# Fewer semaphore updates in a graph network's edge loops, one core of Trainium2

## Chip, cores and metric

One core of a Trainium2 chip runs the whole program as one launch. The metric is the device time of an execution in microseconds (us). The kernel before takes 5689.62 us, the median of three runs (5685.16 to 5692.77). In the text PE is the matrix engine (TensorE), DVE VectorE, ACT ScalarE, POOL GpSimd, SP the engine that starts most plain transfers.

## What is computed

A network of four parts on 3125 nodes with 256 features each. Two of them go over edges:

```python
def _L0_gnn_ref(...):                      # 50000 edges, weight edge_val
    support = input_feature @ weight
    messages = edge_val[:, None] * support[edge_col]
    return segment_sum(messages, edge_row, N_NODES) + bias

def _gat_conv(x, src, dst, W, a_src, a_dst, b, n_nodes):   # edges and one loop a node
    h = (x @ W).reshape(n_nodes, H, C)
    e = leaky_relu((h * a_src).sum(-1)[src] + (h * a_dst).sum(-1)[dst], 0.2)
    ex = exp(e - segment_max(e, dst)[dst])
    alpha = ex / (segment_sum(ex, dst)[dst] + 1e-16)
    return segment_sum(h[src] * alpha[:, :, None], dst).reshape(n_nodes, H * C) + b
```

The first graph layer is a weighted sum over edges. The first feed-forward part chooses among four experts by scores that come from an attention layer of the same form (4 heads, width 16: the "gate"). Then come three attention layers (4 heads of 64) and a last feed-forward part with eight experts. Each part has a layer norm ahead of it and is added to its input.

## The kernel before

The edges are first sorted by destination on the chip (place_edges, place_fine), so that 128 edges at a time, a chunk or column, belong to one bucket of destination nodes. For each column a small table in SBUF holds the number of its bucket.

**sum_edges** (L610) goes over 415 chunks. For each, POOL gathers 128 rows of the table with an indirect transfer (L651) into one of 16 buffers (RS); DVE writes a one-hot matrix times the edge weights (mark, L625) into one of 8 buffers (PS); PE multiplies them (L662) into one of 8 PSUM buffers; DVE adds the result to the bucket's sum in `acc` (take, L631), whose address is a number that DVE loads into a register. Three semaphores say how far each is: `hot` (marks), `summed` (matmuls), `taken` (takes), one update each a chunk. POOL waits for `summed` before it gathers into a buffer again.

**attend_edges** (L665) is the loop of all four attention stages: 72 quads in the gate, 114 in each of the three layers, 414 in all. A quad is four columns (QD = 4). Each engine has its own program, written out in the order in which it runs; a loop body holds six quads (U = 6), with six buffers for gathered rows. For quad q:

- POOL waits until the quad's indices are copied (`staged`) and until quad q - 5 is summed, notes each wait by an own update (`passed`), then issues four gathers (L709).
- DVE fence (L728): waits for ACT's mask, the landed rows and PE's `turned`; subtracts the mask from the rows' scores. The result marks which destination each edge has.
- PE turn (L870): four transposes, then `turned`.
- DVE L757 reduces them to a maximum for each column; L763 scans it to a running maximum, L769 and L774 turn that into the exponent's shift `neg`, L778 into `drop`, by how much an older sum must shrink. Each waits for the one before by `steps`. In between stand the four add_up (L743) of quad q - 2: `acc` times the shrinking factor plus the quad's sums, each waiting for the one before by `taken`, at an address from a loaded bucket number (load_buckets, L732).
- ACT lift (L821): adds the destination's score to the four blocks; stage (L807): copies the indices of quad q + 6; fence (L814): four masks for quad q + 2.
- DVE leak (L748): the leaky relu.
- ACT weigh: four exponentials (L831), each with its own update of `exped`, and a fifth small one (L832), the shrinking factor, with `shrunk`.
- PE turn_back (L878): four transposes, each waiting for its exponential, each with its own update of `turned2`.
- ACT back (L838): waits for all four, copies them from PSUM (`evacd`).
- PE add_rows (L886): 16 small matmuls of weights and gathered rows (each two records in the trace, so x32), then `summed`.

DVE runs fence(q + 1) before the reduce of q; PE runs turn(q + 1) before turn_back(q) and add_rows(q). A stage ends with quads for which POOL has nothing more to gather. No scheduler decides anything: the order on each engine is that of the code.

Of the kernel before, what the change touches and what calls it, by code (L numbers as in the profile page):

```python
# [5 lines left out]
P = 128  # L6
N = 3125
D = 256
# [11 lines left out]
GROUP = 24  # L20
DB = 32
# [111 lines left out]

def place_edges(nc, block, m, name, key_in, val_in, w_in, rec_dram, record, row, bucket):
# [45 lines left out]
    def _(dve):  # L180
# [53 lines left out]
        chain.next(nc.vector.tensor_copy(bucket, ps_bucket))  # L234


def place_fine(nc, block, m, name, key_in, val_in, nch, record, bucket, own_hot, starts, trip_count):
# [45 lines left out]
    def _(dve):  # L283
# [75 lines left out]
        nc.vector.tensor_copy(bucket, ps_bucket)  # L359
        chain.next(nc.vector.tensor_scalar(starts, ps_start, -BIG, None, ALU.mult))  # L360
# [249 lines left out]
def sum_edges(nc, block, m, name, table, rec, index, bucket):  # L610


    hot, summed, taken, cleared = (m.sem(f"{name}_{s}") for s in ("hot", "summed", "taken", "cleared"))
# [4 lines left out]
    part = rec.rearrange("p (c k) -> p c k", k=3)  # L618

    @block.vector  # L620
    def _(dve):
        def mark(c):
            if c >= PS:
                dve.wait_ge(summed, c - PS + 1)
            nc.vector.tensor_scalar(f.hot[c % PS][:, :], m.iota[:, :], part[:, c, 0:1], part[:, c, 2:3], ALU.is_equal, ALU.mult).then_inc(hot, 1)  # L625

        def take(c, b):
            dve.wait_ge(summed, c + 1)
            if c:
                dve.wait_ge(taken, c)  # L630
            nc.vector.tensor_tensor(m.acc[:, b, 0:D], m.acc[:, b, 0:D], ps[c % PS], ALU.add).then_inc(taken, 1)  # L631

        nc.vector.memset(m.acc[:, :, :], 0.0).then_inc(cleared, 1)
        dve.wait_ge(cleared, 1)
        for c in range(PS):
            mark(c)
        for c in range(NCS):
            if c % 4 == 0:
                n = min(4, NCS - c)
                b = nc.values_load_multi_w_load_instructions(bucket[0:1, c:c + n], [mybir.EngineType.DVE], min_val=0, max_val=NT,  # L640
                                                             skip_runtime_bounds_check_because="a bucket's number counts up to 25 buckets")[1]
            take(c, b[c % 4])
            if c + PS < NCS:
                mark(c + PS)

    @block.gpsimd
    def _(pool):
        for c in range(NCS):
            if c >= RS:
                pool.wait_ge(summed, c - RS + 1)  # L650
# [5 lines left out]
    def _(pe):  # L656
        for c in range(NCS):
            pe.wait_ge(hot, c + 1)
            if c >= PS:
                pe.wait_ge(taken, c - PS + 1)  # L660
            pe.wait_ge(landed[c % RS], 16 * (c // RS + 1))
            nc.tensor.matmul(ps[c % PS], f.hot[c % PS][:, :], f.rows[c % RS][:, :], start=True, stop=True).then_inc(summed, 1)  # L662


def attend_edges(nc, block, m, name, width, table, at_dram, nch, lows, rows_in, bucket, own_hot, starts, trip_count):  # L665
# [9 lines left out]
    passed, staged, fenced, masked, turned, reduced, lifted, leaked, top, exped, shrunk, turned2, evacd, summed, taken, steps, acc_in, at_in, tabled, ready = (  # L675
        s_(n) for n in ("passed", "staged", "fenced", "masked", "turned", "reduced", "lifted", "leaked", "top", "exped", "shrunk", "turned2", "evacd", "summed", "taken", "steps",
# [24 lines left out]
    def _(pool):  # L701
        def gather(q, s, first=False):
            pool.wait_ge(staged, q + 1)
            pool.sem_inc(passed, 1)
            if not first:
# [15 lines left out]
    def _(dve):  # L721
        def fence(q, s, turn):

            dve.wait_ge(fenced, q + 1)
            dve.wait_ge(landed[s], turn * (16 * QD) + 16 * QD)
            if not isinstance(q, int) or q >= 2:
                dve.wait_ge(turned, q + (-1))
# [3 lines left out]
        def load_buckets(q):  # L731
            return nc.values_load_multi_w_load_instructions(bucket[0:1, bass.ds(q * QD, QD)], [mybir.EngineType.DVE], min_val=0, max_val=NS - 1,  # L732
                                                            skip_runtime_bounds_check_because="a bucket's number is a sum of one-hot rows times 0 to 99")[1]

        def add_up(q, s, t, b):
            if t == 0:
                dve.wait_ge(shrunk, q + 1)
                dve.wait_ge(summed, q + 1)
            if isinstance(q, int) and q == 0 and t == 0:
                dve.wait_ge(acc_in, 16 * HEADS)  # L740
            if not isinstance(q, int) or q or t:
                dve.wait_ge(taken, q * QD + t)
            nc.vector.scalar_tensor_tensor(acc[:, b, :], acc[:, b, :], f.fac[s][:, t:t + 1], ps_s[s % 2][:, t, :], ALU.mult, ALU.add).then_inc(taken, 1)  # L743
# [6 lines left out]
        def body(q, k, turn, last=None):  # L750
# [8 lines left out]
            if before:  # L759
                add_up(q + (-2), s2, 0, b[0])  # L760
# [3 lines left out]
                                         running[:, bass.ds(q * (2 * QD), 1)], ALU.add, ALU.max).then_inc(steps, 1)  # L764
            if before:
                add_up(q + (-2), s2, 1, b[1])
            neg = f.neg[k]
            dve.wait_ge(steps, q * 3 + 1)
            nc.vector.scalar_tensor_tensor(neg, now.rearrange("p (t k) -> p t k", k=2), -1.0,  # L769
                                           dst[:, bass.ds(q * QD, QD)].unsqueeze(2).to_broadcast([P, QD, 2]), ALU.mult, ALU.subtract).then_inc(steps, 1)  # L770
            if before:
                add_up(q + (-2), s2, 2, b[2])
            dve.wait_ge(steps, q * 3 + 2)
            nc.vector.scalar_tensor_tensor(neg, neg, 0.2, neg, ALU.mult, ALU.min).then_inc(steps, 1)  # L774
            if before:
                add_up(q + (-2), s2, 3, b[3])
            dve.wait_ge(steps, q * 3 + 3)
# [819 lines left out]
```

## Time and profile before

| | us |
|---|---|
| median of 3 runs | 5689.62 (5685.16 to 5692.77) |
| the profiled execution | 5690.18 |
| its span, first to last instruction | 5688.4 |
| PE busy | 2952.8 (52%) |
| DVE busy | 3228.2 (57%) |
| ACT busy | 1883.2 (33%) |
| POOL busy | 2839.1 (50%) |
| mean granted clock of PE | 0.627 |

In time, sum_edges lies at about 1117 to 1716 us (its gathers L651 start from 1117.4 to 1704.4), the gate's loop at about 1836 to 2325, the three layers' loops at about 2800 to 3570, 3665 to 4433 and 4526 to 5296. The sort of the edges comes ahead, the experts between the gate and the first layer and at the end.

How to read the rows further below: a timeline row has the start, the duration, engine, line, operation and tiles, and in brackets how long the engine stood idle ahead of it and what ended that. "remote" stands for a semaphore whose update the trace can't put down to an instruction on this core, "issue" for nothing visible. In a group's row the idle time ahead of all its instructions is added up.

### The profile page before, as it was taken

Reading aid. Unit: us, or ns where it says so; the run is one execution under the profiler, and the core shown is the slowest. Engines: PE = TensorE matmul, PEld = TensorE weight load, DVE = VectorE, ACT = ScalarE, POOL = GpSimd, SP = SyncE. Lnnn points to the kernel's source line nnn. Section 1 sums busy time; section 2 is a strip of 40 time slices with the busy share of each in tenths; the row PEclk is TensorE's granted clock in tenths of the full one; section 3 lists DMA queues with packets and bytes.
Section 4 is the critical chain, followed back from the end, with each engine's and each line's share of the span. In section 5 each row is a group of like instructions: output and inputs, shape, how many; then the busy total and the mean of one; then the engine's idle time right before and its main releaser. Section 6 shows DMA issues by size and latency. Waiting matters only on the chain. (4 is left out here: it accounts for less than half of the span.)

```text
span 5688.4 us, 84219 instructions
## 1 busy us (share of the span) xinstructions
PE 2952.8 (52%) x22141; PEld 1795.1 (32%) x22141; DVE 3228.2 (57%) x8605; ACT 1883.2 (33%) x6577; POOL 2839.1 (50%) x2704
## 2 busy tenths in 40 slices
PE   0235038676554444699455555455555555555274
PEld 0111001133232222477233333333333333333153
DVE  8799999844444444422455555455555455555815
ACT  0000000000001566311266666266666356566310
POOL 2877987266660666100266665166666156665010
PEclk9678569855665555799655555655555655555587
DMA  1000000123331000000333333333333333333000
GB/s 63 27 1 4 0 1 2 50 91 93 93 91 10 8 7 7 19 17 0 80 82 82 82 82 79 77 81 82 81 82 81 69 88 82 82 82 82 9 17 24
DMA packets 201198, 297.75 MB, mean 52 GB/s; under 512 B 110659, under 2 KB 140318, under 8 KB 201022
## 3 DMA queue, kind: packets, MB, share of 16 engines
q0 software_dynamic: 108656, 245.98, 17.4%
q1 hardware_dynamic: 92398, 50.07, 3.5%
q8 instruction: 63, 1.03, 0.1%
q14 instruction: 81, 0.66, 0.0%
HBM read 272.84 MB, written 23.05 MB: 52 GB/s over the span
## 5 line engine op out<-in xcount | busy, mean ns | idle before, releaser
L709 POOL DMA_INDIRECT work<-table_att,work x1368 | 1380.1, 1009 | 1588.5 <-ACT work L807 727.1
L757 DVE TENSOR_REDUCE work<-psum 128x512 f32 (+1 forms) x414 | 286.2, 691 | 1124.6 <-remote 1122.3
L886 PE MATMUL psum<-work 128*32 128x65 f32 (+1 forms) x13248 | 418.3, 295 | 947.4 <-ACT work L838 935.0
L418 POOL DMA_INDIRECT sorted<-stage_rec,stage_row x400 | 675.1, 1688 | 177.1 <-issue 124.0
L878 PE MATMUL psum<-ident,work 128*128 128x128 f32 x1656 | 559.3, 474 | 375.4 <-ACT work L831 278.5
L886 PEld LDWEIGHTS psum<-work 128*32 128x32 f32 x13248 | 331.0, 165 | 1067.6 <-issue 976.9
L831 ACT ACTIVATE work<-work 128x128 f32<-128x128 f32 x1656 | 530.0, 390 | 131.8 <-issue 102.0
L493 ACT ACTIVATE stats<-stats 128x25 f32<-128x25 f32 x5 | 1.1, 223 | 1690.5 <-DVE stats L483 1690.5
L651 POOL DMA_INDIRECT work<-table_sum,index x415 | 395.8, 954 | 278.2 <-SPq L1495 86.1
L838 ACT COPY work<-psum 128x512 f32<-128x512 f32 x414 | 242.2, 585 | 846.2 <-remote 664.6
L821 ACT ACTIVATE work<-psum,work 128x128 f32<-128x128 f32 x1656 | 472.3, 368 | 147.5 <-DVE work L757 130.8
L878 PEld LDWEIGHTS psum<-ident,work 128*128 128x128 f32 x1656 | 301.4, 182 | 677.7 <-ACT work L831 401.3
L662 PE MATMUL psum<-work 128*128 128x256 f32 x830 | 367.0, 572 | 258.8 <-DVE work L625 146.7
L743 DVE SCALAR_TENSOR_TENSOR acc<-acc,work,psum 128x65 f32 (+1 forms) x1656 | 445.9, 269 | 75.5 <-issue 10.8
L870 PE MATMUL psum<-ident,work 128*128 128x128 f32 x1656 | 462.4, 434 | 37.1 <-DVE work L728 28.5
L709 POOL DMA_INDIRECT work<-table_gate,work x288 | 293.4, 1019 | 306.3 <-ACT work L807 131.9
L397 PE MATMUL psum<-work 128*128 128x504 f16 (+1 forms) x1312 | 364.2, 361 | 98.1 <-DVE work L381 41.1
L814 ACT ACTIVATE work<-iota,lows 128x32 f32<-128x32 f32 x1656 | 401.6, 332 | 0.5 <-issue 0.5
L631 DVE TENSOR_TENSOR acc<-acc,psum 128x256 f32 x415 | 174.9, 421 | 317.9 <-PE psum L662 159.0
L870 PEld LDWEIGHTS psum<-ident,work 128*128 128x128 f32 x1656 | 296.3, 217 | 103.4 <-issue 68.0
L662 PEld LDWEIGHTS psum<-work 128*128 128x128 f32 x830 | 190.4, 265 | 435.2 <-DVE work L625 249.0
L728 DVE TENSOR_TENSOR work<-work 128x512 f32<-128x512 f32 x414 | 285.2, 689 | 62.9 <-DMA work<-table_att,work 29.8
(300 smaller groups left out, 4481.8 us busy)
## 6 DMA issues: line engine op xcount, KB each, us to landing
work<-table_att,work POOLq DMA_INDIRECT x1368
table_att<-acc SPq DMA_DIRECT2D x75, 132.0 KB
acc<-table_att SPq DMA_DIRECT2D x12, 812.5 KB
work<-table_sum,index POOLq DMA_INDIRECT x415
sorted<-stage_rec,stage_row POOLq DMA_INDIRECT x400
sorted<-work SPq DMA_DIRECT2D x8, 622.5 KB, 7.9
work<-sorted SPq DMA_DIRECT2D x8, 622.5 KB, 7.7
work<-table_gate,work POOLq DMA_INDIRECT x288
```

What stands on the lines that cost most here:

```text
L397: ins = nc.tensor.matmul(ps[k], row_hot[s][:, k, :], col_hot[s], start=f == 0, stop=f == fc - 1)
L418: nc.gpsimd.indirect_dma_start(out=rec_dram[s * half + f], out_offset=bass.IndirectOffsetOnAxis(ap=m.stage_row[s][:, f:f + 1], axis=0), in ...
L651: nc.gpsimd.indirect_dma_start(out=f.rows[c % RS][:, :], out_offset=None, in_=table, in_offset=bass.IndirectOffsetOnAxis(ap=index[:, c:c + ...
L662: nc.tensor.matmul(ps[c % PS], f.hot[c % PS][:, :], f.rows[c % RS][:, :], start=True, stop=True).then_inc(summed, 1)
L709: nc.gpsimd.indirect_dma_start(out=rows[s][:, t, :], out_offset=None, in_=table[:, 0:rw], in_offset=bass.IndirectOffsetOnAxis(ap=f.index[s ...
L743: nc.vector.scalar_tensor_tensor(acc[:, b, :], acc[:, b, :], f.fac[s][:, t:t + 1], ps_s[s % 2][:, t, :], ALU.mult, ALU.add).then_inc(taken, 1)
L814: ins = nc.scalar.activation(f.pen[s % 2][:, t, :], m.iota[:, 0:DB], ACT.Square, scale=STEP, bias=lows[:, bass.ds(q * QD + t, 1)])
L821: ins = nc.scalar.activation(f.y[s % 2][:, t, :], ps_z[s % 2][:, t * P:(t + 1) * P], ACT.Identity, bias=dst[:, bass.ds(q * QD + t, 1)])
L831: nc.scalar.activation(f.pt[s % 2][:, t, :], f.y[s % 2][:, t, :], ACT.Exp, bias=f.neg[s][:, t, 1:2]).then_inc(exped, 1)
L870: ins = nc.tensor.transpose(ps_z[s % 2][:, t * P:(t + 1) * P], f.z[s % 2][:, t, :, :].rearrange("p h d -> p (h d)"), m.ident[:, :])
L878: nc.tensor.transpose(ps_p[s % 2][:, t * P:(t + 1) * P], f.pt[s % 2][:, t, :], m.ident[:, :]).then_inc(turned2, 1)
L886: ins = nc.tensor.matmul(ps_s[s % 2][DB * h:DB * (h + 1), t, :], f.p[s % 2][:, t, DB * h:DB * (h + 1)], rows[s][:, t, h * w1:(h + 1) * w1] ...
```

## The change

It changes what is announced and when, and moves some steps.

- **attend_edges.** Semaphore updates a quad go from 28 to 17. Gone: `fenced`, `top`, `shrunk`, one of POOL's two `passed`, the update of each quad's `staged` (one update for the six first copies is left), three of four `taken`, three of four `turned2`. The four exponentials keep their own updates and each transpose still waits for its own. What these had covered is covered by other waits and by order: DVE's fence waits for `evacd` of quad q - 2, the drop's small exponential runs ahead of the four large ones, DVE's four add_up wait once.
- ACT does back(q - 1) in the body of quad q, between fence and weigh. PE does add_rows(q - 1) before turn_back(q).
- DVE's waits on `steps` stand ahead of the add_up rather than behind it.
- At a stage's start ACT makes the masks of quads 0 and 1 before it copies the indices of quads 0 to 5.
- The bucket numbers of a quad lie in one word (7 bits each), one load instead of four; in sum_edges six in a word (5 bits each). place_edges and place_fine pack them with five and with twice three more DVE operations.
- **sum_edges.** PE announces two chunks at a time, POOL and DVE wait by pairs, `taken` is gone; the take waits for DVE's own mark instead.

The core of the diff:

```diff
 sum_edges
-            if c >= PS:
-                dve.wait_ge(summed, c - PS + 1)
...
-            dve.wait_ge(summed, c + 1)
-            if c:
-                dve.wait_ge(taken, c)
-            nc.vector.tensor_tensor(m.acc[:, b, 0:D], m.acc[:, b, 0:D], ps[c % PS], ALU.add).then_inc(taken, 1)
+            if c % 2 == 0:
+                dve.wait_ge(summed, c // 2 + 1)
+            dve.wait_ge(hot, last_mark)
+            ins = nc.vector.tensor_tensor(m.acc[:, b, 0:D], m.acc[:, b, 0:D], ps[c % PS], ALU.add)
+            if c + PS >= NCS:
+                ins.then_inc(hot, 1)
...
-                pool.wait_ge(summed, c - RS + 1)
+                pool.wait_ge(summed, (c - RS) // 2 + 1)
...
+            ins.then_inc(summed, 1)
 attend_edges, POOL
-            pool.wait_ge(staged, q + 1)
-            pool.sem_inc(passed, 1)
-            if not first:
+            if first:
+                pool.wait_ge(staged, 1)
+            else:
                 pool.wait_ge(summed, q + (1 - U))
                 pool.sem_inc(passed, 1)
 DVE
-            dve.wait_ge(fenced, q + 1)
+            if not isinstance(q, int) or q >= 3:
+                dve.wait_ge(evacd, q + (-2))
+            elif q == 2:
+                dve.wait_ge(exped, QD)
+            else:
+                dve.wait_ge(staged, 1)
             dve.wait_ge(landed[s], turn * (16 * QD) + 16 * QD)
-            if not isinstance(q, int) or q >= 2:
-                dve.wait_ge(turned, q + (-1))
...
-            return nc.values_load_multi_w_load_instructions(bucket[0:1, bass.ds(q * QD, QD)], [mybir.EngineType.DVE], min_val=0, max_val=NS - 1,
+            word = load_word(dve, nc, bucket[0:1, bass.ds(q * QD, 1)])
+            return [unpack(nc, dve, word, 7, t, NS - 1) for t in range(QD)]
...
             if before:
-                add_up(q + (-2), s2, 3, b[3])
-            dve.wait_ge(steps, q * 3 + 3)
-            nc.vector.tensor_tensor(f.drop[k], neg[:, :, 1], neg[:, :, 0], ALU.subtract).then_inc(top, 1)
+                add_up(q + (-2), s2, 3, b[3]).then_inc(taken, 1)
+            nc.vector.tensor_tensor(f.drop[k], neg[:, :, 1], neg[:, :, 0], ALU.subtract)
 ACT
             act.wait_ge(leaked, q + 1)
-            act.wait_ge(top, q + 1)
-            if not isinstance(q, int) or q >= 2:
-                act.wait_ge(turned2, q * QD + (-QD))
+            nc.scalar.activation(f.fac[s][:, :], f.drop[s], ACT.Exp)
             for t in range(QD):
                 nc.scalar.activation(f.pt[s % 2][:, t, :], f.y[s % 2][:, t, :], ACT.Exp, bias=f.neg[s][:, t, 1:2]).then_inc(exped, 1)
-            nc.scalar.activation(f.fac[s][:, :], f.drop[s], ACT.Exp).then_inc(shrunk, 1)
...
+            if not isinstance(q, int) or q >= 1:
+                back(q + (-1), (k - 1) % U)
             weigh(q, k)
-            back(q, k)
-        for k in range(U):
-            stage(k, k)
         for k in range(2):
             fence(k, k)
+        for k in range(U):
+            ins = stage(k, k)
+        ins.then_inc(staged, 1)
 PE
-                nc.tensor.transpose(ps_p[s % 2][:, t * P:(t + 1) * P], f.pt[s % 2][:, t, :], m.ident[:, :]).then_inc(turned2, 1)
+                ins = nc.tensor.transpose(ps_p[s % 2][:, t * P:(t + 1) * P], f.pt[s % 2][:, t, :], m.ident[:, :])
+            ins.then_inc(turned2, 1)
...
-                pe.wait_ge(taken, q * QD + (-QD))
+                pe.wait_ge(taken, q + (-1))
...
+            if not isinstance(q, int) or q >= 1:
+                add_rows(q + (-1), (k - 1) % U)
             turn_back(q, k)
-            add_rows(q, k)
```

How this stands on two engines, in the loop of the gate (the layers' loop reads alike with wider rows). First PE, one quad of the kernel before. L870 is turn, L878 turn_back, L886 add_rows; ISA and REGISTER_ALU are waits and address arithmetic.

```order
L870 MATMUL psum<-ident,work 128x128 x4
L877 ISA
L878 MATMUL psum<-ident,work 128x128
L877 REGISTER_ALU
L878 MATMUL psum<-ident,work 128x128
L877 REGISTER_ALU
L878 MATMUL psum<-ident,work 128x128
L877 REGISTER_ALU
L878 MATMUL psum<-ident,work 128x128
L883 REGISTER_ALU
L886 MATMUL psum<-work 32x5 x16
```

The same engine and loop in the changed kernel, where L899 is turn, L915 add_rows and L906 turn_back.

```order
L899 MATMUL psum<-ident,work 128x128 x4
L915 MATMUL psum<-work 32x5 x16
L905 ISA
L906 MATMUL psum<-ident,work 128x128
L905 REGISTER_ALU
L906 MATMUL psum<-ident,work 128x128
L905 REGISTER_ALU
L906 MATMUL psum<-ident,work 128x128
L905 REGISTER_ALU
L906 MATMUL psum<-ident,work 128x128
```

The 16 small matmuls now come ahead of the four transposes, and they are those of the quad before.

ACT, one quad of the kernel before, in the same loop: L831 and L832 are the exponentials, L838 back, L821 lift, L814 fence.

```order
L829 REGISTER_ALU
L831 ACTIVATE work<-work 128x128 x4
L832 ACTIVATE work<-work 128x4
L835 REGISTER_ALU
L838 COPY work<-psum 128x512
```

And in the changed kernel, with the end of the fence (L844), back (L864), then the small exponential (L856) and the large ones (L858).

```order
L844 ACTIVATE work<-iota,lows 128x32
L844 ISA
L844 ACTIVATE work<-iota,lows 128x32
L864 COPY work<-psum 128x512
L856 ACTIVATE work<-work 128x4
L858 ACTIVATE work<-work 128x128 x4
```

Back now stands between the fence and the exponentials of the next quad, rather than right behind its own exponentials.

## Rows read from the trace of the kernel before

**Rows 1.** costliest groups, page part 5: busy, mean ns | idle before, releaser
```profile
L709 POOL DMA_INDIRECT work<-table_att,work x1368 | 1380.1, 1009 | 1588.5 <-ACT work L807 727.1
L757 DVE TENSOR_REDUCE work<-psum 128x512 f32 (+1 forms) x414 | 286.2, 691 | 1124.6 <-remote 1122.3
...
L651 POOL DMA_INDIRECT work<-table_sum,index x415 | 395.8, 954 | 278.2 <-SPq L1495 86.1
```

**Rows 2.** 100 us of a layer: busy PE, PEld, DVE, ACT, POOL, then clock, DMA share, GB/s
```profile
3000.00:3100.00 100.00, 52.73 (x612) 34.84 (x616) 52.97 (x168) 61.04 (x227) 60.62 (x61) 0.50 0.32 82
```

**Rows 3.** timeline of one quad: start us, us, engine, line [idle before <-releaser]
```profile
3397.12 0.69 DVE L757 TENSOR_REDUCE work<-psum 128x512 f32 x1 [2.88 <-remote]
3397.13 0.58 ACT L838 COPY work<-psum 128x512 f32<-128x512 f32 x1 [1.99 <-remote]
3397.69 0.95 POOL L709 DMA_INDIRECT work<-table_att,work  x1 [1.35 <-remote]
...
3397.84 1.09 PE L886 MATMUL psum<-work 128*32 128x65 f32 x32 [2.27 <-ACT work L838]
3397.95 1.14 ACT L821 ACTIVATE work<-psum,work 128x128 f32<-128x128 f32 x4 [0.24 <-DVE work L757]
...
3398.87 1.12 PE L870 MATMUL psum<-ident,work 128*128 128x128 f32 x4
...
3399.05 0.97 ACT L814 ACTIVATE work<-iota,lows 128x32 f32<-128x32 f32 x4
...
3400.92 1.35 PE L878 MATMUL psum<-ident,work 128*128 128x128 f32 x4 [0.93 <-ACT work L831]
3401.47 0.95 POOL L709 DMA_INDIRECT work<-table_att,work  x1 [0.30 <-issue]
...
3403.73 0.69 DVE L757 TENSOR_REDUCE work<-psum 128x512 f32 x1 [2.79 <-remote]
...
3404.30 0.95 POOL L709 DMA_INDIRECT work<-table_att,work  x1 [1.87 <-remote]
```

**Rows 4.** timeline, VectorE at the end of the last layer
```profile
5278.29 0.68 DVE L757 TENSOR_REDUCE work<-psum 128x512 f32 x1
...
5287.07 0.69 DVE L757 TENSOR_REDUCE work<-psum 128x512 f32 x1 [0.67 <-PE psum L870]
```

**Rows 5.** timeline of a chunk of sum_edges
```profile
1400.73 0.95 POOL L651 DMA_INDIRECT work<-table_sum,index  x1 [0.47 <-PE psum L662]
...
1402.05 0.42 DVE L631 TENSOR_TENSOR acc<-acc,psum 128x256 f32 x1 [0.76 <-PE psum L662]
1402.17 0.95 POOL L651 DMA_INDIRECT work<-table_sum,index  x1 [0.49 <-PE psum L662]
```

**Rows 6.** timeline around a pause of POOL in the last layer
```profile
5185.16 1.17 POOL L709 DMA_INDIRECT work<-table_att,work  x1 [1.85 <-issue]
5185.43 0.69 DVE L757 TENSOR_REDUCE work<-psum 128x512 f32 x1
...
5186.92 0.58 ACT L838 COPY work<-psum 128x512 f32<-128x512 f32 x1 [0.54 <-PE psum L878]
...
5189.85 1.35 PE L878 MATMUL psum<-ident,work 128*128 128x128 f32 x4
...
5192.92 0.95 POOL L709 DMA_INDIRECT work<-table_att,work  x1 [0.30 <-issue]
5195.51 0.69 DVE L757 TENSOR_REDUCE work<-psum 128x512 f32 x1 [5.32 <-remote]
```

**Rows 7.** timeline at the start of the first layer
```profile
2799.19 0.67 ACT L807 COPY work<-sources 128x4 int32<-128x4 int32 x6 [5.29 <-PEq L1495]
...
2799.76 1.80 ACT L814 ACTIVATE work<-iota,lows 128x32 f32<-128x32 f32 x8
...
2831.33 0.95 POOL L709 DMA_INDIRECT work<-table_att,work  x1 [0.30 <-issue]
2834.41 0.69 DVE L757 TENSOR_REDUCE work<-psum 128x4 f32<-128x512 f32 x1 [6.72 <-remote]
```

## What the change should do, said before it ran

> **What bounds the kernel now.** I read the list of costliest groups first. It has two entries that don't fit together: the four edge stages' gathers on POOL (L709) are busy 1380.1 us in the attention layers with 1588.5 us of idle time ahead of them, and VectorE's reduce L757 is idle 1124.6 us, 1122.3 of it put down to "remote" [rows 1]. So neither the gather engine nor the engine that uses the rows is full: they wait for each other, or for something between them. The windows say how steady this is: in 100 us of a layer POOL is busy 60.62, PE 52.73, DVE 52.97, ACT 61.04, at a granted clock of 0.50, the 1.2 GHz level [rows 2].
>
> Then one quad from release to release [rows 3]. L757 starts at 3397.12 and 3403.73: 6.61 us. ACT's L838 starts beside it both times and POOL's first gather 0.57 us later. POOL: three starts 1.26 apart (3397.69 to 3401.47 is 3.78), 0.95 for the last, which ends at 3402.42, and then 1.88 idle; 3.78 + 0.95 + 1.88 = 6.61. The other engines are done before that: PE's L870 (the turn that L757 reads) ran at 3398.87 to 3399.99, L878 (which L838 reads) ended at 3402.27, and still L757 starts only at 3403.73. So PE's announcements aren't seen when PE's work ends. They are seen by DVE, ACT and POOL together, 1.31 us after POOL's last gather ended. That POOL's work is what they are held behind shows at a stage's end, where no gathers are left: L757 at 5278.29 and, two quads on, at 5287.07, 4.39 us a quad with the same arithmetic [rows 4].
>
> How long they are held after POOL's last gather goes with how many semaphore updates ACT, DVE, PE and POOL made since POOL last stood idle (counted in the code: 28 a quad, 3 a chunk in sum_edges). Three places:
> - sum_edges, 3 updates: POOL ends at 1401.68, DVE's take starts at 1402.05, 0.37 later [rows 5];
> - a regular quad, 28 updates: 1.31 [rows 3];
> - about every 24 quads POOL pauses by itself (idle 1.85 "issue"), updates come through, and it then runs seven gathers in a row; about 40 updates lie in that run: end 5193.87, L757 at 5195.51, 1.64 [rows 6]. At a layer's start, 24 gathers and some 50 updates: 2832.28 to 2834.41, 2.13 [rows 7].
>
> (1.31 - 0.37) / 25 is 0.038 us an update, (1.64 - 1.31) / 12 is 0.028. I take 0.034.
>
> **The change, part by part.**
>
> *Fewer updates, attention loop.* 28 become 17 a quad: DVE 11 to 7, ACT 9 to 6, PE 6 to 3, POOL 2 to 1. If the hold is shortened as above it goes from 1.31 to 1.31 - 11 x 0.034 = 0.94, so 0.37 us a quad (bounds 0.31 to 0.42, and nothing, if the count is not the cause). L757 waited for "remote" 380 times; 380 x 0.37 = 141 us, bounds 118 to 160. The rest of the period (0.57 + 3.78 + 0.95) stays, since each quad still has four gathers.
>
> What would be late next: in the new order ACT does back(q-1) after lift(q), the index copy and the fence, and PE does turn_back(q) behind add_rows(q-1). Counted from the release at L757: lift, L807 and L814 end at 3400.02, that is +2.90 [rows 3]; back 0.58 to about +3.5; L886 1.09 to +4.7; ACT's small exponential and the four large ones (1.28) to about +5.0; the last transpose 0.53 behind it, +5.5 (in the kernel before: 3402.27 - 3397.12 = +5.15). POOL ends at +5.30 and the new release would be at +6.24. So the lengthened chain still fits, with 0.7 us to spare, and costs nothing as long as POOL's end sets the release. With that cover gone it costs 0.35 us a quad.
>
> DVE's waits for its own scan and steps now stand ahead of the add_ups rather than behind them; queued behind them are the add_ups, L748 and the next fence L728. Gaps of this kind are about 0.1 us, four a quad; DVE has 2.8 us to spare before each release [rows 3], so nothing here. Three of four bucket loads go, in the same idle time: nothing.
>
> *sum_edges.* One chunk takes 1402.17 - 1400.73 = 1.44 us: 0.95 gather and 0.49 idle [rows 5]. With one announcement for two chunks the second gather follows the first after 0.30 or 0.31, as L709's do: 0.95 + 0.31 + 0.95 + 0.49 = 2.70 for two, against 2.88. 199 pairs x 0.18 = 36 us. Bounds: nothing, to 415 x (1.44 - 1.26) = 75 if POOL no longer stops at all. I take 36.
>
> *Starts.* The index copies L807 come behind the eight fences L814, 1.80 us [rows 7]; POOL's first gather waits for them. 4 stages x 1.8 = +7. Bounds 0 to 9.
>
> *Ends.* Six quads a stage run with POOL done. There ACT's back no longer waits for the turn_back just ahead of it (0.54 idle at 5186.92, [rows 6]), which may give 0.3 back; DVE's four own waits may take 0.4. 24 quads: -7 to +10, I take 0.
>
> *Packing* the bucket numbers: eleven small DVE operations, well under 0.3 us each with their waits: +3, once.
>
> Sum: 5690.2 (the profiled execution, 5688.4 of it the span) - 141 - 36 + 7 + 3 = 5523; it lies 0.6 above the median of the runs, so 5522.
>
> **A rule against it.** The rows hold an announcement longer where more were made. By the Trainium skill, VectorE: DVE Perf Modes, section "The DRAIN you can't avoid", a semaphore after each of eight copies cost nothing over one after the last (13.88 us both); by that, all that is removed from DVE and ACT is worth nothing, and only the pairs and the starts are left. The page measured one engine alone, with no gathers beside it; no row here shows the hold change at a constant gather count except by comparing different stages. The Trainium skill, TensorE: Matmul & The Clock Gate, section "The cost: per-tile semaphore tail", has increments of PE serialize at 26.3 ns each; by it, three fewer a quad would be an estimated 0.079 x 414 = 33 us.
>
> **The rivals.**
>
> *A: PE's announcements come through while POOL works.* In [rows 6] L757 at 5185.43 and L838 at 5186.92 start while POOL gathers, and POOL goes on to four more gathers without stopping, so one quad's six PE updates (turned, four turned2, summed) passed; then nothing until POOL stops, L757 idle 5.32. In the regular quad six are let through together at the release and none after. If six is what passes per stop, three a quad means two quads per stop: 7 x 1.26 + 0.95 + 0.57 + a hold of 1.31 + 6 x 0.034 = 1.51 gives 11.85 for two, 5.93 a quad. 380 x (6.61 - 5.93) = 258; sum_edges between 36 and 75; 5690 - 258 - 55 + 10 = 5387, between 5340 and 5430. For: the six, at both places. Against: it asks for a count of PE's alone, when the hold's length seems to go with everybody's.
>
> *B: the count of updates does not matter,* the hold grows with the length of POOL's run, which differs in all of these places too (one gather, four, seven, 24). Then sum_edges and the starts alone: 5690 - 36 + 10 = 5664, between 5625 and 5690. Against: from 4 to 24 gathers the hold grows only by 0.82, from 1 to 4 by 0.94, so it isn't in proportion to gathers; the updates explain it more evenly.
>
> *C: no more holding at all,* POOL never stops: 4 x 1.26 = 5.04 a quad, 380 x 1.57 = 597, 5690 - 597 - 75 + 10 = 5028. Only if a small number of updates is never held; [rows 5] has a hold with 3 a stop, which speaks against it.
>
> *D: slower.* In the kernel before PE's last transpose (3402.27) and POOL's last gather (3402.42) end 0.15 us apart, so one regular quad can't tell which of them the release is counted from. If it is PE's end, or the later, the longer chain on ACT and PE decides: +5.5 instead of +5.15, with a hold that doesn't shrink. 380 x 0.35 = +133, -36 + 10: 5797; with 0.2 us later only (5.5 against POOL's 5.30) 5740. It decides from the point where turn_back's end passes POOL's, which by my sum it does by 0.2. Against: at 5189.85 to 5191.20 PE was done and the release came at 5195.51, 1.64 behind POOL [rows 6].
>
> **How the numbers follow.** Forecast (hold shrinks with the count, 5490 to 5560) 0.37; A 0.25; B 0.17; C 0.06; D 0.15. A measurement of this kernel can't tell less than about 0.2% (11 us) from no change. Faster: the forecast, A, C and most of B (5664 is 26 below, but its upper end is inside 0.2%), 0.75; same, 0.09; slower, 0.16 (D and the upper end of the unknown costs). The range takes in the forecast, A and B: 5340 to 5690; outside are C and D. The forecast's own range is 5490 to 5560.
>
> **What the profile after would show.** Right: L757 starts every 6.2 us, POOL's idle ahead of a quad's first gather 1.5 us instead of 1.88, the four gathers as before, L651 in pairs (idle 0.3, then 0.49). A shows as eight gathers in a row and a long "remote" wait of L757 at every second quad; B as 6.6 again with fewer updates; D as L757 following PE's L906 (turn_back), not POOL's end. I'd be wrong in the mechanism, whatever the time, if the idle time of POOL ahead of a quad stays at 1.88 or if it follows something other than POOL's own last gather.

## The result: no gain where POOL stops, 1.1% where it doesn't

The changed kernel takes 5699.27 us (median of 20 runs, 5696.77 to 5702.61), the kernel before beside it 5689.77 (20 runs, 5684.97 to 5693.85 but for a slow one of 6042.44). The ratio is 1.0017, 95% interval 1.0011 to 1.0024: 0.1 to 0.2% slower, where 5522 was forecast. Its profiled execution has a span of 5695.0 us against 5688.4.

The list of groups by line of the changed kernel (busy, mean ns | idle before, releasers), to set beside [rows 1]:

```profile
L733 POOL DMA_INDIRECT work<-table_att,work x1368 | 1405.1, 1027 | 1555.1 <-ACT work L837 729.8 <-remote 481.6 <-issue 343.7
...
L763 DVE SCALAR_TENSOR_TENSOR acc<-acc,work,psum 128x65 f32 (+1 forms) x1656 | 448.9, 271 | 1289.7 <-remote 903.7 <-DVE work L788 121.6 <-DVE work L794 118.9
...
L777 DVE TENSOR_REDUCE work<-psum 128x512 f32 (+1 forms) x414 | 282.6, 683 | 0.9 <-remote 0.9
```

POOL's idle time ahead of the layers' gathers is 1555.1 us and was 1588.5, and the gathers themselves take 1405.1 us and took 1380.1. VectorE's wait has only moved: L777, the reduce, which stood 1124.6 us as L757, waits 0.9 us, and the add_up (L763) waits 1289.7, since now it is the first on VectorE to need `summed`. One quad in the timeline, to set beside [rows 3]:

```profile
3400.25 0.28 DVE L763 SCALAR_TENSOR_TENSOR acc<-acc,work,psum 128x65 f32 x1 [2.19 <-remote]
...
3400.81 0.95 POOL L733 DMA_INDIRECT work<-table_att,work  x1 [1.86 <-remote]
...
3404.01 1.36 PE L906 MATMUL psum<-ident,work 128*128 128x128 f32 x4 [2.11 <-issue]
3404.59 0.95 POOL L733 DMA_INDIRECT work<-table_att,work  x1 [0.30 <-issue]
...
3406.78 0.28 DVE L763 SCALAR_TENSOR_TENSOR acc<-acc,work,psum 128x65 f32 x1 [2.13 <-remote]
...
3407.33 0.95 POOL L733 DMA_INDIRECT work<-table_att,work  x1 [1.79 <-remote]
```

From release to release it is 6.53 us here (3400.25 to 3406.78) and was 6.61 there. PE's turn_back ends at 3405.37, POOL's last gather at 3405.54, the add_up starts at 3406.78: a hold of 1.24 with 17 updates, where 1.31 went with 28 and 0.94 was forecast. One quad can mislead, since in both kernels the stops have two lengths, about 1.35 and 1.85 us. Over the three layers they are 324 in each kernel, and average 1.57 us in the changed one and 1.68 before; the forecast was a cut of 0.37.

In sum_edges the stops became fewer, the pace stayed. POOL now mostly gathers 14 or 16 chunks on end and then stops for up to 3.6 us; here is such a stop:

```profile
1402.97 0.95 POOL L673 DMA_INDIRECT work<-table_sum,index  x1 [0.60 <-issue]
1404.23 0.95 POOL L673 DMA_INDIRECT work<-table_sum,index  x1 [0.30 <-issue]
...
1407.94 0.95 POOL L673 DMA_INDIRECT work<-table_sum,index  x1 [2.76 <-DMA x<-in_x_dram]
```

The single gathers with 0.49 of idle time [rows 5] are only one of the patterns of the kernel before. It has 102 idle times over 0.4 us, and from 1411 us on it too gathers 19 to 21 chunks on end and stops for up to 3.76 us; this gather ends such a stop:

```profile
1594.23 0.95 POOL L651 DMA_INDIRECT work<-table_sum,index  x1 [3.75 <-DMA x<-in_x_dram]
```

The changed kernel has 35 such idle times, and both come to the same time: first to last gather 586.9 us before, 588.5 after (415 gathers, 1.42 each).

Where the 6.6 us of the span come from, by the starts of the first and last gather of each stage:

| stretch | before | after | difference |
|---|---|---|---|
| to the first L651/L673 | 1117.4 | 1122.9 | +5.5 |
| gathers of sum_edges | 586.9 | 588.5 | +1.6 |
| from there to the gate's first | 132.2 | 142.0 | +9.8 |
| the gate's gathers | 467.5 | 465.8 | -1.7 |
| the three layers' | 747.1, 746.0, 746.7 | 740.6, 745.0, 741.9 | -12.3 |
| between the later stages and behind them | 1144.6 | 1148.1 | +3.6 |

The 9.8 lie behind the last gather: the last take (L631) starts 11 us after it in the kernel before, and in the changed one (L653, at 1731.4 against 1711.5) 20 us after it. How many chunks a run of gathers leaves waiting would explain that; it was not tested.

### The profile page after: what moved, and what is told of

It reads as the page before. It is cut to its first block and busy times, and to the rows that moved or that the text cites. A ratio compares the mean times of both kernels' runs of the same rounds, so it can differ in the third digit from the quotient of the medians.

```text
span 5695.0 us, 84123 instructions
## 1 busy us (share of the span) xinstructions
PE 2882.4 (51%) x22141; PEld 1777.3 (31%) x22141; DVE 3219.2 (57%) x8616; ACT 1840.5 (32%) x6577; POOL 2870.6 (50%) x2704
## 5 line engine op out<-in xcount | busy, mean ns | idle before, releaser
L733 POOL DMA_INDIRECT work<-table_att,work x1368 | 1405.1, 1027 | 1555.1 <-ACT work L837 729.8
L763 DVE SCALAR_TENSOR_TENSOR acc<-acc,work,psum 128x65 f32 (+1 forms) x1656 | 448.9, 271 | 1289.7 <-remote 903.7
L906 PE MATMUL psum<-ident,work 128*128 128x128 f32 x1656 | 560.0, 473 | 818.9 <-ACT work L858 699.5
L439 POOL DMA_INDIRECT sorted<-stage_rec,stage_row x400 | 663.7, 1659 | 177.2 <-issue 124.3
L915 PE MATMUL psum<-work 128*32 128x65 f32 (+1 forms) x13248 | 419.2, 295 | 538.7 <-ACT work L864 516.4
L906 PEld LDWEIGHTS psum<-ident,work 128*128 128x128 f32 x1656 | 300.6, 182 | 1046.3 <-ACT work L858 775.1
L915 PEld LDWEIGHTS psum<-work 128*32 128x32 f32 x13248 | 330.3, 165 | 703.6 <-ACT work L864 482.3
L673 POOL DMA_INDIRECT work<-table_sum,index x415 | 396.1, 954 | 280.9 <-issue 103.3
L858 ACT ACTIVATE work<-work 128x128 f32<-128x128 f32 x1656 | 525.8, 389 | 0.0
L899 PE MATMUL psum<-ident,work 128*128 128x128 f32 x1656 | 444.0, 422 | 52.8 <-DVE work L755 41.4
L856 ACT ACTIVATE work<-work 128x4 f32<-128x4 f32 x414 | 86.4, 209 | 1015.6 <-issue 797.4
L844 ACT ACTIVATE work<-iota,lows 128x32 f32<-128x32 f32 x1656 | 404.9, 334 | 26.9 <-PEq L1526 20.9
L653 DVE TENSOR_TENSOR acc<-acc,psum 128x256 f32 x415 | 174.9, 421 | 306.2 <-issue 193.6
L899 PEld LDWEIGHTS psum<-ident,work 128*128 128x128 f32 x1656 | 311.5, 218 | 79.4 <-DVE work L755 49.3
L684 PEld LDWEIGHTS psum<-work 128*128 128x128 f32 x830 | 163.1, 244 | 470.5 <-DVE work L646 349.0
L1285 PE MATMUL psum<-xt,work 128*128 (+1 forms) x960 | 267.3, 437 | 74.1 <-ACTq L1324 44.5
```

The source lines that it names most:

```text
L439: nc.gpsimd.indirect_dma_start(out=rec_dram[s * half + f], out_offset=bass.IndirectOffsetOnAxis(ap=m.stage_row[s][:, f:f + 1], axis=0), in ...
L673: nc.gpsimd.indirect_dma_start(out=f.rows[c % RS][:, :], out_offset=None, in_=table, in_offset=bass.IndirectOffsetOnAxis(ap=index[:, c:c + ...
L684: ins = nc.tensor.matmul(ps[c % PS], f.hot[c % PS][:, :], f.rows[c % RS][:, :], start=True, stop=True)
L733: nc.gpsimd.indirect_dma_start(out=rows[s][:, t, :], out_offset=None, in_=table[:, 0:rw], in_offset=bass.IndirectOffsetOnAxis(ap=f.index[s ...
L763: return nc.vector.scalar_tensor_tensor(acc[:, b, :], acc[:, b, :], f.fac[s][:, t:t + 1], ps_s[s % 2][:, t, :], ALU.mult, ALU.add)
L844: nc.scalar.activation(f.pen[s % 2][:, t, :], m.iota[:, 0:DB], ACT.Square, scale=STEP, bias=lows[:, bass.ds(q * QD + t, 1)])
```

## The experiments

Runs fell on several chips, and each is compared with the kernel before on its own chip. That turned out to matter: on three of them (5689, 5743 and 5736 us for the kernel before) POOL stops as in [rows 3]; on two (5083 and 5081 us) it never does. The first eight runs are on chips with stops. Each chip was seen in one group of runs only.

**More updates, no more instructions.** In ACT's fence and lift and PE's turn and add_rows, each by the same pattern:

```diff
-            ins.then_inc(fenced, 1)
+                ins.then_inc(fenced if t == QD - 1 else more_act, 1)
```

> The kernel before, with 12 more semaphore updates a quad on instructions that are there anyway (six on ACT's lift and fence, six on PE's turn and add_rows); no instruction is added and nothing waits for them. The theory of the prediction (the hold goes with the number of updates, 0.034 us each): 12 x 0.034 x 380 quads = +155 us, about 5845, and L757 starts every 7.0 us. The new theory, that a gather costs 1.331 us and each instruction that the trace records costs 0.0079 us while POOL gathers, whatever it announces: no change, 5690.

Measured: 5698.2 against 5689.3, ratio 1.0013 (1.0003 to 1.0023). Twelve updates more a quad cost 9 us, not 155. The count of updates isn't what the hold is owed to. The gathers' row says more, beside L709 in [rows 1] with 1380.1 busy and 1588.5 idle:

```profile
L710 POOL DMA_INDIRECT work<-table_att,work x1368 | 1317.8, 963 | 1657.2 <-ACT work L808 728.8 <-remote 588.9 <-issue 339.5
```

The gathers are 62 us shorter and the idle time 69 us longer: what stays, to within 7 us, is the sum of the two, not the stop.

**An idle engine.** On SP, in each of the three layers:

```diff
+            with sp.Fori(0, 200) as i:
+                for _ in range(40):
+                    sp.wait_ge(acc_in, 16 * HEADS)
```

> The kernel before, with SP, idle during the layers, running a loop of 8000 waits that are satisfied already in each of the three attention layers (40 waits, 200 times). No engine waits for SP there. Theory of updates: no change, 5690. Theory of instructions (0.0079 us each for every engine's): 24000 x 0.0079 = +190 us, about 5880, if all engines' instructions share what is short; no change if only those of PE, DVE and ACT do.

Measured: 5799.9, ratio 1.0192 (1.0174 to 1.0211). Forecast were +190 us, if every instruction costs 7.9 ns, or nothing. The row of that line (times recorded, duration ns min/median/max), with 20 waits in each round of the loop and not 40:

```profile
L702 SPq EVENT_SEMAPHORE  x12000: 1/28/723, 2830.5 to 5404.4; - x197
```

A wait that is long satisfied takes 28 ns, and up to 723. In the timeline the long ones lie where POOL gathers: SP runs one every 0.06 us, until 0.3 to 0.7 us after a quad's first gather has started; from then until 0.4 to 0.9 us after the last has ended, most steps take 0.70 to 0.73. So it isn't PE alone that is held. Nor is it every engine: the address arithmetic of VectorE's add_up in the changed kernel, on a chip with stops, is never stretched.

```profile
L763 DVEq ALU_OP  x2898: 40/45/51, 1887.4 to 5302.7; - x194
```

The gathers of a layer took 754 us against 747, so the 3160 to 3440 waits that SP ran beside them (and a tenth as many loop instructions) cost 7 us, about 2 ns each; the rest of the 110 us lies outside the gathers (between the layers 136 and 134 us instead of 118 and 115, and the end), where SP's loop still runs and others wait for SP.

**Fewer instructions on PE.**

```diff
-                for h in range(HEADS):
+                for h in range(1 if nch == NCF else HEADS):
```

> The kernel before; in the three layers add_rows computes one head of four: 4 matmuls a quad and not 16, so 12 matmuls of 0.07 us each less on PE, which is idle 40% of a quad. The sums of the other heads are left out. Updates are the same. Theory of updates, or of POOL's own time: no change, 5690. Theory of instructions: 12 matmuls are 48 records of a quad's 156 (two passes, each with a weight load), 342 quads x 48 x 0.0079 = -130 us, about 5560.

Measured: 5650.2, ratio 0.9929 (0.9911 to 0.9947); 16416 records less for 39 us are 2.4 ns each, where 7.9 was expected. Timeline of POOL:

```profile
3044.31 0.95 POOL L709 DMA_INDIRECT work<-table_att,work  x1 [0.30 <-issue]
...
3049.34 0.95 POOL L709 DMA_INDIRECT work<-table_att,work  x1 [4.08 <-PE psum L886]
...
3058.34 0.95 POOL L709 DMA_INDIRECT work<-table_att,work  x1 [0.30 <-issue]
```

POOL now runs eight gathers (3049.34 to 3058.34) and then stops 4.08 us rather than four and 1.87. `summed` came through in the middle of the run, which is the pattern of rival A, and it gained 39 us only. Passing an announcement early doesn't pay here: what was not waited for is waited for later.

**The two halves of the change.** With sum_edges, its table and place_edges of the kernel before, and the reverse:

> The changed kernel with sum_edges and its table of bucket numbers as before; the attention loops are the changed ones. From the stage times of the two traces: the changed kernel's sums cost 5.5 us in packing, 1.6 in the loop and 9.8 behind it, the attention loops give 13.5 back. So 5699 - 17 = 5682, 8 below the kernel before. By the prediction's steps it would be near 5560.

> The kernel before with the changed sum_edges and its packed bucket numbers; the attention loops are as before. The other half of the run att_new_sum_old: from the stage times +5.5 for packing, +1.6 in the loop, +9.8 behind it: 5706. By the prediction's steps 36 below the kernel before, 5657.

Measured: 5687.1 against 5689.3, ratio 0.9997 (0.9988 to 1.0006); and 5759.3 against 5743.1, ratio 1.0028 (1.0017 to 1.0039). The new sums cost 16 us, as the stage table has it (16.9), and the attention half by itself brings nothing that can be told from zero: its gathers take 13.7 us less, 3.6 of them go in packing ahead of the sums and 5.7 between and behind the stages (1150.3 us against 1144.6), and the rest in stretches whose code is the same.

**Pauses between gathers.** POOL clears an unused tile between the gathers of a quad:

```diff
             for t in range(QD):
+                if t and nch == NCF:
+                    nc.gpsimd.memset(f.spare[:, :], 0.0).then_inc(spare, 1)
+                    pool.wait_ge(spare, q * 3 + t)
+                    pool.sem_inc(passed, 1)
```

> The kernel before; in the layers POOL clears a small unused tile between the four gathers of a quad and waits for that, which keeps it from gathering for some tenths of a us three times a quad (g each). If the hold is a delay that begins when the last gather ends, the period grows by the whole of it: with g = 0.3 by 0.9 us a quad, +300 us or more. If gathers leave a debt that is worked off whenever POOL doesn't gather, wherever the pause lies, the stop ahead of a quad shrinks from 1.86 us by what the pauses are long, and the time stays near 5690.

Measured: 5960.7 against 5743.1, ratio 1.0379 (1.0361 to 1.0398). The forecasts were +300 us or more for a delay that starts when a gather ends, and no change for a debt; +218 is neither, so the timeline has to tell. POOL:

```profile
3204.84 0.96 POOL L714 DMA_INDIRECT work<-table_att,work  x1 [0.80 <-POOL work L711]
...
3206.76 0.96 POOL L714 DMA_INDIRECT work<-table_att,work  x1 [0.79 <-issue]
3208.03 0.96 POOL L714 DMA_INDIRECT work<-table_att,work  x1 [0.30 <-issue]
```

The pauses became 0.96 us (memset, wait, restart), 0.66 more than the usual 0.30, so 2.0 a quad. And the stop ahead of a quad is gone: 3206.76 is the last gather of one, 3208.03 the first of the next, 0.30 apart. The gathers of a layer took 835 us, 7.33 a quad, against 6.65 on that chip (758.4 us a layer for the same loops in sum_new_att_old): 0.68 more for 2.0 of pauses. The other 1.3 are the stop that they stand in for. So the stop is no delay that begins when a gather ends; it is time that POOL's gathers need in sum, and it may lie anywhere.

The trace of the kernel before says the same, ahead of any experiment. These are the two rows of POOL just ahead of [rows 3]:

```profile
3393.62 1.46 POOL L709 DMA_INDIRECT work<-table_att,work  x1 [0.31 <-issue]
3395.38 0.95 POOL L709 DMA_INDIRECT work<-table_att,work  x1 [0.30 <-issue]
```

One gather of this quad took 1.46 us, and the stop behind it, ahead of 3397.69, is 1.35; the next quad has none that long, and a stop of 1.87. In the 297 regular quads of the layers, 145 have a stop under 1.6 us, on average 1.39 behind 4.29 us of gathering; the other 152 have 1.87 behind 3.82. The sum is 5.68 or 5.69 either way, with the same 28 updates: a gather that is held up for another reason pays towards the stop.

**Three gathers of four.**

```diff
-            for t in range(QD):
+            for t in range(QD if nch != NCF else 3):
```

> The kernel before; in the layers POOL issues three gathers a quad rather than four (the fourth column computes on stale rows, so its sums are left out); instructions and updates of the other engines are the same. If the stop is the debt of the gathers, 0.31 us each, it shrinks with them: 6.55 x 3/4 = 4.91 a quad, 330 x 1.64 = -541, about 5150. If it is owed to the other engines' instructions or updates, it stays 1.86 and only a gather's 1.26 goes: 5.29 a quad, -416, about 5275.

Measured: 5257.8 against 5743.1, ratio 0.9155 (0.9139 to 0.9172). A layer's gathers took 594.5 us, 5.22 a quad. One gather less would bring 6.65 to 5.39 by its own 1.26; another 0.17 went with it. The 485 us lie between the two forecasts (541 and 416). So by this estimate about 4 x 0.17 = 0.7 of the 1.3 belongs to the gathers and 0.6 to what the other engines do. In sum_edges, with little beside a gather, 0.16 a gather is all there is (1.42 - 1.26).

**Attention loop alone, without the packed numbers and with the old start.**

> Only the attention loop's order and updates are new: sum_edges, the tables of bucket numbers and their loads as before, and at a stage's start the index copies again ahead of the masks. Against the run att_new_sum_old (5687) this takes away 3.6 us of packing and 4 x 1.5 to 1.8 us of later starts: 5678, 0.2% below the kernel before. By the prediction's hold theory about 5550.

Measured: 5708.9 against 5743.1, ratio 0.9942 (0.9928 to 0.9955), 34 us faster and more than expected. The trace counts instructions (compute, register, wait, each pass of a matmul): per gather, over the middle 72 quads of each layer, 38.9 in the kernel before, 38.4 in the changed one, 36.7 here. The packed word's shifts and masks cost VectorE 7 recorded instructions a quad more than the three loads that it saves.

**More and fewer instructions.** Eight `act.sem_inc(spare, 1)` ahead of weigh and four behind it; and the loops written out for the trips that the edge count makes certain, on all four engines:

```diff
+        for i in range(plain):
+            for k in range(U):
+                body(i * U + (U + k), k, i + 1)
-        with dve.Fori(0, trips) as i:
+        with dve.Fori(plain, trips) as i:
```

> The kernel before with 12 instructions more a quad on ACT, each of which does nothing but add one to a semaphore that nobody waits for. The run more_updates had the same number of updates on instructions that were there anyway and took 0.13% (0 to 0.2%) more. If only updates count: the same, 0.1%. If an instruction costs 8 to 9 ns of the time in which POOL stands still, whatever it does (slope between the traces of before, changed and att_new_rest_old): 12 x 0.0085 x 380 = +39 us and the updates' 9 us on top, +0.8%.

> The kernel before, with 300 of the 414 quads written out rather than run in a loop (the trips that the edge count makes certain); the rest stays a loop. Every compute instruction, wait and semaphore update is the same, in the same order; the register instructions that work out addresses and counts go, some 32 a quad over all engines. Theory of updates, or of POOL's own time: no change. Theory of instructions: 300 x 32 x 0.0085 = -82 us, -1.4%. The longer code could also have to be waited for.

> The kernel att_new_rest_old (0.6% under the kernel before) with the same 300 quads written out. The two gains add up if both are instructions: about 2% under the kernel before. If the attention loop's gain came from somewhere else it may be less.

> The changed kernel again, beside the others on the same chip: within 0.1 to 0.3% above the kernel before, as measured, if its result doesn't depend on the chip.

These four fell on a chip without stops. Measured: 0.9999 (0.9990 to 1.0009), 0.9919 (0.9902 to 0.9936), 0.9994 (0.9984 to 1.0004) and 0.9888 (0.9871 to 0.9904), with 5083.1 us for the kernel before. The groups of POOL in the layers, first of more_instructions, whose time is that of the kernel before:

```profile
L710 POOL DMA_INDIRECT work<-table_att,work x1368 | 1368.8, 1001 | 1132.3 <-ACT work L808 715.5 <-issue 401.4 <-PE psum L891 15.4
```

and of the changed kernel on the same chip:

```profile
L733 POOL DMA_INDIRECT work<-table_att,work x1368 | 1320.0, 965 | 1139.0 <-ACT work L837 723.0 <-issue 411.5 <-PE psum L915 4.6
```

No "remote" is left among the releasers, and the idle time is 1132 to 1139 us: 4 x 0.30 us a quad and the gaps between the stages. POOL gathers without a stop, in either kernel. The changed one is 55 us faster there since a gather takes 965 ns on average and not 1001 (with the gate's, 976 and not 1014: 1656 x 0.038 = 63 us). Most take 0.95. Of the layers' 1368, 187 take 1.1 to 1.5 us, and 143 of these run beside VectorE's leaky relu, where of the shorter ones a third does (394 of 1181); in the changed kernel 42 are that long. att_new_rest_old_2 below, which has the new order but four loads a quad, has 1017 ns, so the order alone doesn't bring it. That the leaky relu is what lengthens them is argued from this, not shown.

The same line of the take's address arithmetic in sum_edges, on a chip with stops and on this one (register instructions, duration ns min/median/max):

```profile
L653 DVEq ALU_OP  x760: 1/45/1392, 1132.4 to 1731.2; - x190
```

```profile
L653 DVEq ALU_OP  x760: 40/45/64, 1131.5 to 1651.9; - x190
```

> The kernel before with 12 more instructions a quad on ACT, again. On the chip of the last four runs POOL never stood still (kernel before 5083 us) and these instructions cost nothing (ratio 0.9999). On a chip that shows the stops (kernel before near 5690 or 5740): theory of instructions +0.8%, theory of updates and any other +0.1%. On one without stops: nothing again.

> The kernel before with 300 quads written out, again. Without stops it was 0.8% faster (0.9919). On a chip with stops: theory of instructions -82 us, ratio 0.986, with POOL's stop ahead of a quad shorter by 0.27 us; if instructions don't matter to the stops, no change, since POOL's gathers and stops set the time there.

On a chip with stops: 5758.0 against 5736.0, ratio 1.0036 (1.0022 to 1.0050), and 5698.8 against 5736.0, ratio 0.9934 (0.9917 to 0.9950). 4968 instructions more for 22 us are 4.4 ns each, or 2.6 without the 9 us that as many updates cost in more_updates; 9450 fewer (31.3 a gather, and not 38.9) for 37 us are 3.9 ns. So instructions count there, at a third to half of the expected price. With 4 ns for all, 39 x 4 x 0.004 = 0.6 a quad would be what three_gathers left over; with the 2.4 ns of one_head for PE's half of them it is 0.5. But without stops more_instructions costs nothing.

> The kernel att_new_rest_old with 300 quads written out, again. On a chip with stops, from the two halves measured there (0.9942 and 0.9934): 0.988 if their gains add up. On the chip without stops it was 0.9994.

> The kernel att_new_sum_old (changed attention loops with packed bucket numbers, sums as before) with the 300 quads written out. With stops: more register instructions for unpacking than best_unrolled (7 a quad), so 0.990 against its 0.988. Without stops, if the packed load is what kept POOL's gathers at 0.96 us there: about 0.987.

> Only the attention loop's order and updates new, again, beside after_again_2. With stops: 0.994, as before. Without stops: between 0.989 and 1.0, as POOL's mean gather tells.

> The changed kernel again. On a chip with stops 1.0017, as first measured; on one without stops 0.989.

These came to a chip without stops again: 0.9984 (0.9975 to 0.9994), 0.9892 (0.9876 to 0.9909), 0.9996 (0.9986 to 1.0005), 0.9892 (0.9876 to 0.9909), against 5081.5 us. The changed kernel's result does depend on the chip, twice 1.1% faster without stops. The packed loads, a small loss with stops, are what it is owed to without: in the layers they are all that tells after_again_2 from att_new_rest_old_2 but for the starts, and POOL's mean gather is 964 ns in the one and 1017 in the other (975 in new_unrolled). It is not their number as such: before_unrolled, with four loads a quad, has 986. The one version seen faster than the kernel before on both kinds of chip is before_unrolled (0.9919 and 0.9934), the kernel before with its loops written out. Whether the gains of best_unrolled add up on a chip with stops stays open.

## Why the prediction was wrong, step by step

- **What bounds the kernel.** Right as far as it went: PE's announcements are seen late, behind POOL's gathers, and POOL's gathers and stops set the pace. But the views showed one chip; without stops the kernel before is 607 us faster. That the changed kernel takes 5028 us there, as rival C has it, is luck: the chip took the stops away, not the change, which is worth 55.
- **The hold goes with the updates, 0.034 us each.** This step failed. The three places it was fitted to differ in updates, in gathers and in all other work at once, so the fit couldn't tell them apart. Its own row had the objection: the quad ahead of the one it was read from stopped for 1.35 us and not 1.87, with the same 28 updates [rows 3]. More_updates gives 9 us where it says 155. And the hold isn't a delay: by spaced it is time owed, by estimate 0.17 us for each gather and 2 to 4 ns for each instruction of the others. At more_updates' 1.8 ns the 11 updates less a quad are worth 8 us, and 0.5 instructions less a gather 1656 x 0.5 x 0.004 = 3; the attention loops' gathers gave 14, of 141. The sign that the prediction named for a wrong mechanism, idle time that stays at 1.88 ahead of a quad, is there: 1.86 and 1.79 in the rows above.
- **sum_edges, -36.** Wrong twice. One chunk was taken for all 415, where the kernel before has only 102 idle times over 0.4 us; that its 1.44 us is near the mean of 1.42 is luck. And the stops became fewer and longer, at the same pace: +1.6 in the loop. Behind it came +9.8, which the prediction didn't have.
- **Starts, +7; packing, +3.** Measured: between and behind the stages +3.6, all told, and about 1 of the 9.8. Ahead of the sums +5.5; 3.6 are there with the attention's packing alone (att_new_sum_old). In the code each packing step waits for the one before.
- **The longer chain on ACT and PE costs nothing.** Right: turn_back ends at 3405.37, 0.17 ahead of POOL's last gather. Forecast were +5.5 from the release; it is 5.12 in this quad.
- **The rivals.** B had it right that the count doesn't matter and gave 5664, because it kept the gain in sum_edges; that the hold grows with POOL's run was its other half, and only the gathers' share of the debt bears it out. A's pattern is seen in one_head, without its gain. D, the slower one, named the wrong mechanism: the small loss came from sum_edges' end and the packing.
- **The rule against it.** The Trainium skill, VectorE: DVE Perf Modes, section "The DRAIN you can't avoid", has a semaphore after each of eight copies on VectorE cost nothing. More_updates, which adds its updates on ScalarE and TensorE, agrees nearly: 4968 updates for 9 us are 1.8 ns each. It deserved more than the 0.17 of rival B.

## What to carry to other kernels

A wait that follows an engine's end by a varying time should not be priced by what is being changed until something else that varies with it (gathers, instructions) is held fixed in a comparison, and first over all the quads of the trace at hand: one quad and one chunk misled twice here. Where a stop's length changes with its frequency so that the pace stays, it is a debt: look for what it is owed for, not for whom it ends. And such a cost may belong to the chip it is measured on, so the kernel should be measured on another one before work goes into it.

## What was not expected of the hardware

- The same kernel takes 5690 to 5743 us on three chips and 5081 to 5083 on two. With stops, SP's satisfied waits (28 ns) and the register instructions of sum_edges (45 ns, L653) are in part stretched to 0.7 us, 1392 ns at most, while VectorE's address arithmetic in the attention loops takes 51 ns at most (L763); on a chip without stops L653 takes 64 ns at most. What makes the difference isn't shown. That the stops grow a little with the instructions of other engines, even of one that computes nothing, and that of the changed kernel's semaphore updates (landings of gathers included) 10.7 a gather are recorded in its layers with stops and 19.8 without, points to something that is written for each instruction and shares a path with POOL's gathers; that is argued, not shown. The recording of the trace is itself written for each instruction. Every execution here was recorded, so whether POOL would stop without the recording is open too.
- Writing out the loop of register-addressed bodies gains 0.7 to 0.8% for the kernel before on both kinds of chip; 7.6 of 38.9 recorded instructions a gather were address arithmetic. Without stops it can't be the price of instructions, since 4968 more cost nothing there; what it is isn't shown, and in the new order with four loads a quad it gains 0.15% there (best_unrolled_2, 5072.8 us, against att_new_rest_old_2, 5080.4).
